# A DLRM tower on one core: a pipeline of steps with TensorE results used one step later, one-sample products in 32-column matmuls, and PSUM scratch for the reciprocals

## The reference

```python
e = stack([tbl_f[ids[:, f]] for f in range(26)], axis=1)      # 2048 x 26 x 64, a gather
x = layer_norm(dense_t @ Wd.T, gd, bd)                        # 2048 x 128
y = layer_norm(einsum('bnd,ed->bne', e, Ws), gs, bs)          # 2048 x 26 x 128
y = layer_norm(einsum('bne,pn->bep', y, Wsi), gsi, bsi)       # 26 rows mixed to 32, normed over the 32
T = concatenate([x[:, None], swapaxes(y, 1, 2)], axis=1)      # 33 vectors of 128 a sample
Z = einsum('bnd,bmd->bnm', T, T)                              # all pairs; the lower triangle is used
z = layer_norm(Zflat @ Wl.T, gl, bl)[:, :384]
h = relu(concatenate([z, dense_t]) @ W_top1 + b_top1)         # 640 -> 512
h = relu(h @ W_top2 + b_top2)                                 # 512 -> 256
out = h @ W_top3                                              # 256 -> 1
```

## Time and profile before

| | us |
|---|---|
| median of 3 runs | 692.35 |
| lowest and highest of them | 689.19 and 695.31 |
| the profiled execution, whole | 694.04 |
| its span in the profile | 692.1 |
| TensorE clock granted, mean over the span | 0.968 of full |

### The profile page before, as it was taken

How to read it: one execution, slowest core, us unless ns; L and a number is a source line. 1 busy time by engine, 2 the same in 40 slices (tenths; PEclk the granted TensorE clock), 3 DMA queues, 4 the chain that set the end, 5 groups by cost and what they waited for, 6 DMA issues and landing times.

```text
span 692.1 us, 9152 instructions
## 1 busy us (share of the span) xinstructions
PE 599.8 (87%) x3275; PEld 448.1 (65%) x3275; DVE 468.7 (68%) x680; ACT 308.9 (45%) x677; POOL 427.8 (62%) x420
## 2 busy tenths in 40 slices
PE   0447779888999899998999899998999899989777
PEld 0425656656777677876776677767686677656645
DVE  4266886958786768677777878676876877786100
ACT  1112454535455545545454554544454545454211
POOL 5777777777777777777777777777777720000000
PEclk9979999989999999999999999999999999999979
DMA  7811121111212121212112111212121200000000
GB/s 230 311 25 25 26 48 30 45 30 26 53 25 68 26 52 24 67 26 52 28 35 56 33 45 25 67 26 52 26 52 26 52 11 11 17 18 10 27 1 0
DMA packets 28540, 31.23 MB, mean 45 GB/s; under 512 B 9928, under 2 KB 20944, under 8 KB 28112
## 3 DMA queue, kind: packets, MB, share of 16 engines
q0 software_dynamic: 13312, 13.66, 10.1%
q1 hardware_dynamic: 15168, 16.99, 7.4%
q10 hardware_dynamic: 16, 0.01, 0.0%
HBM read 23.28 MB, written 0.01 MB: 34 GB/s over the span
## 4 chain that ended last, share of the span: by engine, by line
PE 57%; POOL 15%; DVE 12%; issue 9%; ACT 6%; DMA 1%; SPq 1%; ACTq 0%
POOL emb L248 15%; PE bank_z L367 11%; PE bank_m L402 11%; PE bank_h L379 10%; PE bank_y L353 7%; PE bank_u L342 5%; PE bank_t L327 5%; PE bank_m L410 4%; DVE tt L796 3%; DVE tt L813 2%; DVE ssum L803 2%; PE bank_t L319 2%; ACT sq L533 1%; PE bank_m L418 1%; ACT zbig L550 1%
## 5 line engine op out<-in xcount | busy, mean ns | idle before, releaser
L248 POOL DMA_INDIRECT emb<-in_tables,ids x416 | 427.6, 1028 | 130.3 <-issue 126.2
L367 PEld LDWEIGHTS bank_z<-tt 128*128 128x128 f32 x1024 | 136.1, 194 | 56.3 <-issue 32.6
L367 PE MATMUL bank_z<-tt 128*128 128x136 f32 x1024 | 161.4, 292 | 5.5 <-DVE tt L813 5.2
L550 ACT COPY zbig<-bank_z 128x408 f32<-128x408 f32 (+1 forms) x192 | 98.0, 511 | 137.6 <-PE bank_z L367 137.6
L803 DVE TENSOR_REDUCE ssum<-sq 128x32 f32<-128x1024 f32 x64 | 128.0, 2000 | 28.4 <-ACT sq L533 27.2
L796 DVE TENSOR_TENSOR tt<-bank_y,biasc 128x512 f32<-128x512 f32 x128 | 82.2, 684 | 86.0 <-PE bank_y L353 86.0
L379 PE MATMUL bank_h<-wz,zr 128*128 128x512 f32 x224 | 103.1, 601 | 3.9 <-ACT zr L557 3.9
L327 PEld LDWEIGHTS bank_t<-gram_w,embt 128*128 128x128 f32 x416 | 60.0, 209 | 43.2 <-ACT embt L518 31.1
L327 PE MATMUL bank_t<-gram_w,embt 128*128 128x128 f32 x416 | 65.8, 302 | 23.1 <-ACT embt L518 23.1
L342 PE MATMUL bank_u<-mix_w,emb 128*128 128x192 f32 (+4 forms) x512 | 81.8, 303 | 0.0
L813 DVE TENSOR_TENSOR tt<-tt,srs 128x1024 f32<-128x1024 f32 x64 | 78.4, 1225 | 2.2
(11 more groups left out here) (93 smaller groups left out, 494.0 us busy)
## 6 DMA issues: line engine op xcount, KB each, us to landing
emb<-in_tables,ids POOLq DMA_INDIRECT x416, 2.4
zs<-zbig SPq DMA_DIRECT2D x64, 70.0 KB
zs<-zbig SPq DMA_DIRECT2D x64, 42.0 KB
dense<-in_dense SPq DMA_DIRECT2D x8, 256.0 KB, 5.7
zbig<-in_wfull SPq DMA_DIRECT2D x1, 2048.0 KB, 10.8
wz<-in_wrows SPq DMA_DIRECT2D x1, 1792.0 KB, 14.4
w<-in_w SPq DMA_DIRECT2D x1, 1280.0 KB, 10.2
w<-in_w SPq DMA_DIRECT2D x1, 512.0 KB, 11.5
```

The costliest lines, as they stand in the source:

```text
L248: pool.indirect_dma_start(emb[:, e, t, D * a:D * a + D], None, x_in["tables"], bass.IndirectOffsetOnAxis(ap=ids[:, col:col + 1], axis=0),) ...
L367: mm = pe.matmul(bank_z[at % 2][:, o:o + 4 * ZC], quad[:, 4 * C0:4 * ZC], quad, start=True, stop=True)
L550: act.copy(zbig[:, u % 2, :, C0:CZ, g0:g0 + q1 - q0], bank_z[at % 2][:, 0:4 * ZC * (q1 - q0)].rearrange("p (g c j) -> p j c g", j=4, c=ZC) ...
```

## The change

The lags and the order on each engine are written anew, and these pieces change with them:

- `gram` writes a bank of its own, `bank_g`; it runs a step after `turn` (TURN_AT = 2, GRAM_AT = 3), and `times_e`, `reduce_e` and `scale_e` a step after that (SCALE_AT = 4). `project` is at 5, the chain `add_bias` to `scale_t` at CHAIN_AT = 6, `products` at PROD_AT = 7 and `products_out` at ZOUT_AT = 8.
- GROUPS is (4, 3, 3, 3), and the variance of each group is reduced, rooted and scaled by itself.
- Both reciprocals go to `bank_g` in PSUM and are read from there by `scale_e` and `scale_t`; for that `gram` waits for `scale_t` and `scale_e` of the same step.
- `products` makes one matmul a sample: 32 stationary columns by 34 moving columns, four samples into the four groups of 32 partitions of the one `bank_z`. `tt` is laid out a sample at a time, so that `sum_s` reads contiguous numbers. `products_out` is one copy a chunk, and `products` waits for the copy of the chunk before.
- `flat` and `top1` are cut into three pieces on three steps. For the last superunit `open_last` does the dense part of `top1` ahead on four banks, and `close_last` adds the rest.
- The wait of the gathers is unchanged in the code (`mixed` of the unit three before); what is smaller is the distance between `turn` and `mix` of a chunk, two steps instead of four.

```diff
-GROUPS = ((0, 4), (4, 8), (8, 12), (12, 13))
-PARTS = ((0, 8), (8, 13))
-QUADS = ((0, 3), (3, 6), (6, 8))
+GROUPS = ((0, 4), (4, 7), (7, 10), (10, 13))
+PIECES = ((0, 3), (3, 5), (5, 7))
-A_AT, MIX_AT, PROJ_AT, PROD_AT = 0, 4, 5, 6
-MOVE_AT, FLAT_AT, NORM_AT, TURNZ_AT = 10, 11, 13, 13
-TOP1A_AT, TOP1B_AT, TOP2_AT, TOP3_AT = 18, 21, 22, 25
+TURN_AT, GRAM_AT, SCALE_AT, MIX_AT, PROJ_AT, CHAIN_AT, PROD_AT, ZOUT_AT = 2, 3, 4, 4, 5, 6, 7, 8
+XCOL_AT, MOVE_AT, FLAT_AT, TURNZ_AT, GAINZ_AT = 6, 11, 13, 16, 17
+DENSEX_AT, TURNX_AT, SUMX_AT = 1, 2, 3
+TOP1_AT, TOP2_AT, TOP3_AT = (22, 23, 24), 28, 29
...
-        tt = sb("tt", [P, 2, 32, ZC, 4])
+        tt = sb("tt", [P, 2, UNIT, ZC])
...
             def turn(u, k):
-                after(pe, prod_ok, 4 * u + k)
+                after(pe, embt_ok, 4 * u + k)
...
             def gram(u, k):
                 pe.wait_ge(embt_ok, 4 * u + k + 1)
+                after(pe, t_ok, 4 * u + k + GRAM_AT - CHAIN_AT + 1)
+                after(pe, scaled, 4 * u + k + GRAM_AT - SCALE_AT + 1)
...
-            def products(u, h, i):
-
-                if i == 0:
-                    pe.wait_ge(t_ok, 4 * u + h + 1)
-                    pe.wait_ge(xcol_ok, u + 1)
-                at = 12 * u + 3 * h + i
-                after(pe, zc_ok, at - 1)
-                q0, q1 = QUADS[i]
-                for q in range(q0, q1):
-                    o = 4 * ZC * (q - q0)
-                    quad = tt[:, u % 2, 8 * h + q, :, :].rearrange("p c j -> p (c j)")
-                    mm = pe.matmul(bank_z[at % 2][:, o:o + 4 * ZC], quad[:, 4 * C0:4 * ZC], quad,
-                                   start=True, stop=True)
+            def products(u, h):
+                pe.wait_ge(t_ok, 4 * u + h + 1)
+                pe.wait_ge(xcol_ok, u + 1)
+                after(pe, zc_ok, 4 * u + h)
+                for g in range(2 * GRP // 4):
+                    for j in range(4):
+                        one = tt[:, u % 2, 2 * GRP * h + 4 * g + j, :]
+                        mm = pe.matmul(bank_z[PR * j:PR * j + PR, ZC * g:ZC * g + ZC], one[:, C0:ZC], one,
+                                       start=True, stop=True)
                 mm.then_inc(z_done, 1)
...
+            def open_last():
+                pe.wait_ge(y_ok, 8 * NU)
+                pe.wait_ge(u_ok, 4 * NU)
+                pe.wait_ge(embt_ok, 4 * NU)
+                for c in range(4):
+                    for t in (3, 4):
+                        pe.matmul(last_banks[c][:, 0:SUP], w1[:, t, P * c:P * c + P],
+                                  dense[:, LAST % DB, t - 3, :], start=(t == 3), stop=False)
...
             def scale_t(u, h):
                 dve.wait_ge(sstd_ok, 4 * u + h + 1)
-                dve.reciprocal(srs[:, h % 2, :], sstd[:, h % 2, :]).then_inc(srs_ok, 1)
+                after(dve, prod_ok, min(4 * u + h + CHAIN_AT - SCALE_AT + 1, 4 * NU))
+                srs = bank_g[:, 0:2 * GRP]
+                dve.reciprocal(srs, sstd[:, h % 2, :]).then_inc(srs_ok, 1)
```

More of the change, by code:

```diff
@@ L454, in _ @@
             for s in range(STEPS):
-                late(s)
-                now, mi, pj, pd = chunk(s, A_AT), chunk(s, MIX_AT), chunk(s, PROJ_AT), chunk(s, PROD_AT)
-                if pj:
-                    project(*pj)
-                if pd:
-                    products(*pd, 0)
-                if mi:
-                    mix(*mi)
-                if pd:
-                    products(*pd, 1)
-                if now:
-                    turn(*now)
-                u = unit(s, FLAT_AT)
-                if u is not None:
-                    flat(u, range(0, 4))
-                u = unit(s, FLAT_AT + 1)
-                if u is not None:
-                    flat(u, range(4, SLOTS))
-                j = sup(s, TOP1A_AT)
-                if j is not None:
-                    top1(j, 0)
-                j = sup(s, TOP1B_AT)
-                if j is not None:
-                    top1(j, 1)
-                if now:
-                    gram(*now)
-                if pd:
-                    products(*pd, 2)
+                c = chunk(s, PROD_AT)
+                if c:
+                    products(*c)
+                c = chunk(s, PROJ_AT)
+                if c:
+                    project(*c)
+                c = chunk(s, TURN_AT)
+                if c:
+                    turn(*c)
+                if s == OPEN_AT:
+                    top2(LAST - 1)
+                    open_last()
+                for piece in range(3):
+                    u = unit(s, FLAT_AT + piece)
+                    if u is not None:
+                        flat(u, piece)
+                    j = top1_of(s, piece)
+                    if j is not None:
+                        top1(j, piece)
+                if s == CLOSE_AT:
+                    close_last()
+                j = top3_of(s)
+                if j is not None:
+                    top3(j)
+                j = top2_of(s)
+                if j is not None and s != OPEN_AT:
+                    top2(j)
+                i = sup(s, DENSEX_AT)
+                if i is not None:
+                    dense_x(i)
+                i = sup(s, TURNX_AT)
+                if i is not None:
+                    turn_x(i)
+                i = sup(s, SUMX_AT)
+                if i is not None:
+                    sum_x(i)
                 u = unit(s, TURNZ_AT)
@@ L487, in _ @@
                     turn_z(u)
-                j = sup(s, TOP2_AT)
-                if j is not None:
-                    top2(j)
-                i = dense_x_of(s)
-                if i is not None:
-                    dense_x(i)
-                i = turn_x_of(s)
-                if i is not None:
-                    turn_x(i)
-                i = sum_x_of(s)
-                if i is not None:
-                    sum_x(i)
-                j = sup(s, TOP3_AT)
-                if j is not None:
-                    top3(j)
+                c = chunk(s, MIX_AT)
+                if c:
+                    mix(*c)
+                c = chunk(s, GRAM_AT)
+                if c:
+                    gram(*c)
+                late(s)
         @block.scalar
@@ L612, in relu1, with relu_last @@
                 ins.then_inc(h1_ok, 1)
+            def relu_last():
+                act.wait_ge(top2_done, LAST)
+                for c in range(4):
+                    act.wait_ge(last_done, c + 1)
+                    ins = A(h1[:, c, :], last_banks[c][:, 0:SUP], ACT.Relu, bias=b1c[:, c:c + 1])
+                ins.then_inc(h1_ok, 2)
             def relu2(j):
@@ L629, in _ @@
             for s in range(STEPS):
-                now, mi, pj, pd = chunk(s, A_AT), chunk(s, MIX_AT), chunk(s, PROJ_AT), chunk(s, PROD_AT)
-                if pd:
-                    products_out(*pd, 0)
-                u = unit(s, 3)
-                if u is not None:
-                    root_e(u, 0)
-                u = unit(s, 5)
+                c = chunk(s, PROJ_AT)
+                if c:
+                    mixed_out(*c)
+                c = chunk(s, ZOUT_AT)
+                if c:
+                    products_out(*c)
@@ L656, in _ @@
-                j = sup(s, TOP1B_AT)
-                if j is not None:
-                    relu1(j, 1)
-                if pd:
-                    products_out(*pd, 2)
-                u = unit(s, MOVE_AT)
+                c = chunk(s, CHAIN_AT)
+                if c:
+                    squares(*c)
+                c = chunk(s, SCALE_AT)
+                if c:
+                    root_e(*c)
+                c = chunk(s, CHAIN_AT)
+                if c:
+                    root_s(*c)
+                u = unit(s, XCOL_AT)
```

309 lines of the change are left out of this document (155 added, 154 removed).

## The result

The changed kernel takes 613.82 us (611.81 to 617.47) where the kernel before takes 691.85 in the same comparison: a ratio of 0.888, 95% interval 0.882 to 0.894. The forecast was 660. The sign holds, the size does not: 78 us are gained and not 32, and the time is that of rival (2), 612. The execution profiled after took 614.92 us, 613.1 of them its span; the one before has 692.1 of span, so the two profiles differ by 79.0 us.

What follows compares the result with a forecast made beforehand. The prediction took PE to bound the kernel: 179 us to chunk 20, 43 steps x 9.3 (400) and a tail of 80 gave 659 us of span, 660 as a median. Its own range was 645 to 676, for 8 in 10 610 to 712.

Steps and rivals of the forecast that it cites:

- rival (2): In `products`, the four column groups run together, 8 to 16 ns a record; gathers then bind; 612 us; chance 0.2.
- The price of a small record: In `products`, each load hides behind the matmul before it: 32 ns a record, 2.05 us for a chunk's 64.
- the lower bound: In `products`, four column groups might run together as `project`'s row halves do, down to 8 ns a record.
- PE's step: Steady part: PE sets the pace in all steps but the one with `norm_x`, 9.3 us a step against 9.43.
- The slope: A record's cost in `products` weighs 64 x 51 steps: 1 ns is 3.3 us, and at 42 ns the gain is gone.
- The new wait: `products` waits for the previous chunk's `products_out`, queued behind `mixed_out` on ACT: 0.35 us a step, plus 0.1 for changing tiling.
- `times_e`, `gram` and DVE in lock step: DVE and PE meet once a step, through `times_e`, `gram` and `scale_t`; DVE's step is 6.4 us, about 6.9 with hand-overs.
- rival (3): A late ACT copy delays `products`, the next `gram` and `times_e`: 0.7 us a step more, 690 us; chance 0.14.
- The gathers: On POOL, 1.25 us each instead of 1.33, since no tensor_tensor of the loop has both inputs in SBUF.
- The start: Up to `turn` of chunk 20, 138 gathers are due: 4.3 + 138 x 1.25 + 2.4 = 179 us.
- The tail: From the last `turn` to the end: 80 us, 13.5 less than before, 6.5 of it by `open_last`.
- Rival (1): In `products`, load and matmul of so few columns do not overlap: 60 ns a record, 764 us; chance 0.18.

Runs made afterwards that it cites:

- the run in a row: The changed kernel with the two loops of `products` exchanged, so the eight samples of one column group follow each other: 657.47 us, ratio 0.949.
- the copy first: The changed kernel with ACT's copy of the products ahead of its copy of `mix` instead of behind it: 611.66 us, ratio 0.883.

## Why the prediction was wrong

- **The price of a small record: the step that failed.** "I take 32 ns, nearest to the one row with a small load: 64 x 0.032 = 2.05 us a chunk." Measured: 10.7 ns and 0.68 us. The row chosen (one-column loads, one after the other in one group) was a good witness for records in one group, which take 27.0 ns. It was no witness for this order, in which each sample goes to another group than its neighbours. The prediction had the row that was, two row halves of `project` running together in the earlier trace rows, and used it for the lower bound and rival (2) instead of for the forecast. The choice should have followed the loop: `j` runs innermost, so neighbouring samples never share a group.
- **PE's step.** 9.3 us forecast, 8.17 measured. With 27 ns it is 9.05 measured and 9.0 by the sum, so the rest of this sum is right to 0.1.
- **The slope.** "1 ns is 3.3 us": from 27.0 to 14.6 ns the time falls by 35.6 us, 2.9 a ns; from there to 10.7 by 8.0, 2.1 a ns. It is lower where gathers and copies begin to bind. At the full slope the forecast would have come to 590, too low.
- **The new wait.** 0.35 us a step forecast for `products` behind ACT's copy; 2.5 in eight steps measured, 0.31 each. The change into the column tiles is 0.09 a step (0.205 us behind `gram` instead of 0.111). Missing is the wait of `turn` for the copy out of `bank_t`, 0.7 in eight steps; it is nothing in the run in a row and comes with the fast products. The 0.52 us between the last record of `project` and `turn` are not missing: they are part of the 1.06 a chunk that the sum has for `project`.
- **`times_e`, `gram` and DVE in lock step.** DVE has 52.2 us of work in eight steps, 6.5 each (6.4 forecast), and PE hardly waits for it: rival (3) is not borne out.
- **The gathers.** 1.25 each, as forecast, and it was the source in PSUM. Rival (2) said that they would bind at 8.1 a step; the steady part of the changed kernel is at 8.17 for another reason, and only with the copy first does it run at the gathers' pace. So rival (2) had the mechanism of the records right, and its total in part by luck.
- **The start.** 179 forecast, 181.4 measured; 15 of these us are the gathers', since half of them leave 166.6.
- **The tail.** 80 forecast, 78.6 measured, but one of its parts was wrong. "6.5 of it by `open_last`" is nothing, because "20.2, which hides the move of the products" was taken as cover up to its end: the copy behind the move was over 11.5 us before PE got to `flat`. That the sum is right to 1.4 us is luck in part: its three pieces, 34.7, 20.2 and 25.1 (21.6 and 3.5), measure 29.6, 21.8 and 27.2.
- **Rival (1)**, 60 ns a record, is not borne out. The slower side exists all the same: the kernel is 27% slower on the chips where records come in slowly. That is not rival (1)'s reason, since a chunk that is not interrupted takes 0.76 us there too.

## What to carry to other kernels

Where small matmuls can go to different column or row groups of the array, put neighbours in the instruction stream on different groups; the same 64 records took 0.68 us in turn and 1.70 in a row. Price a new kind of record by a row in which neighbours share what the new ones will share, and when a term falls well below its forecast, look at what it used to cover: here a copy on ACT, and then the gathers. Work that is put ahead of a transfer's end as cover has to be no longer than the transfer. And a kernel with twice the instructions may depend more on the chip that it lands on; why it did here is open.

## What the runs showed of the hardware

- The column groups of TensorE work at the same time: loads of 32 and matmuls of 34 columns in fp32 start every 27.0 ns on the mean in one group, every 14.6 in two, every 10.7 in four (8.9 in the fastest chunks, and where they come in parts of 16 or 24).
- A whole-array record starts 0.52 us behind a 512-column record in a row half of the array (0.985 us in the median where the granted clock was 0.788). A record of 34 columns in a column group starts 0.205 us behind a whole-array one of 128, where whole-array ones are 0.11 apart.
- A VectorE multiplication with both sources in SBUF lengthens a gather that begins inside it on GpSimd from 0.94 to 1.91 us; with one source in PSUM it stays at 0.94.
- On disturbed chips PE got a few small records each 0.7 us after a good start of some 45. Kernels with 6347 matmul records and all gathers took 307 to 506 us more there than elsewhere (the changed one 486), the one with 3275 about 170 to 200. With half of the gathers the changed kernel took 269 more; why the gathers matter for this was not tried.
